# One attention and feed-forward block on one core: batch 1's projections behind the first scores, paired products in the spare bank, idle products, another order at the end

## What is computed

```python
x = x + xattn(layernorm(x), ctx)
x = x + ffn(layernorm(x))

def xattn(x, ctx):
    q, k, v, qc = x @ Wq + bq, x @ Wk + bk, x @ Wv + bv, x @ Wcq + bcq
    kc, vc = ctx @ Wck + bck, ctx @ Wcv + bcv
    y  = softmax(causal(q @ k.T * scale)) @ v        # per head
    y += softmax(qc @ kc.T * scale) @ vc
    return y @ Wp + bp

def ffn(x):
    w = top8(sigmoid(x @ Wr + br)), normalized       # [tokens, 32]
    shared = (silu(x @ Wg_s + bg_s) * (x @ Wu_s + bu_s)) @ Wd_s + bd_s
    routed = sum over e of w[:, e] * ((silu(x @ Wg[e] + bg[e]) * (x @ Wu[e] + bu[e])) @ Wd[e] + bd[e])
    return shared + routed
```

## Time and profile before

| | before |
|---|---|
| median of 3 runs | 218.98 us (217.91 to 220.17) |
| the profiled execution | 220.7 us |
| its span, first to last instruction | 218.4 us |
| its mean granted TensorE clock | 0.944 |
| busy: PE, DVE, ACT, POOL | 197.5, 165.4, 141.4, 94.2 us |
| share of the chain that ended last: PE, DVE, ACT, issue | 69%, 15%, 6%, 5% |

### The profile page before, as it was taken

One profiled execution on the slowest core, in us unless ns is written; L12 is line 12 of the kernel. 1 busy time (PEld: TensorE's weight loads), 2 busy tenths in 40 slices (PEclk: granted clock), 3 DMA queues, 4 the chain that ended last, 5 costly groups with the idle time before them and its releaser, 6 DMA issues.

```text
span 218.4 us, 3993 instructions
## 1 busy us (share of the span) xinstructions
PE 197.5 (90%) x1227; PEld 143.5 (66%) x1238; DVE 165.4 (76%) x378; ACT 141.4 (65%) x275; POOL 94.2 (43%) x148
## 2 busy tenths in 40 slices
PE   7884989898999999899898978679999999999983
PEld 2553776566776767676665646457888888887752
DVE  2988766367677898798765689796687887887982
ACT  3456465568689888898777693665567656555471
POOL 7799555024237365737646322524265233220000
PEclk9998555899999999999999999999999999999996
DMA  4264422102343324210211100000023000000003
GB/s 115 81 161 128 107 66 70 32 12 72 78 104 79 85 62 103 48 41 3 72 36 39 36 0 2 3 0 0 2 56 91 18 2 0 0 0 3 0 0 96
DMA packets 20433, 10.39 MB, mean 48 GB/s; under 512 B 11881, under 2 KB 18542, under 8 KB 20414
## 3 DMA queue, kind: packets, MB, share of 16 engines
q1 hardware_dynamic: 19290, 9.24, 16.8%
q0 software_dynamic: 672, 0.69, 1.3%
q10 hardware_dynamic: 452, 0.23, 0.5%
HBM read 4.51 MB, written 0.52 MB: 23 GB/s over the span
## 4 chain that ended last, share of the span: by engine, by line
PE 69%; DVE 15%; ACT 6%; issue 5%; POOL 2%; DMA 1%; DVEq 0%; POOLq 0%; ACTq 0%
PE psum L1268 12%; PE psum L1269 10%; PE psum L1270 10%; PE psum L1370 6%; PE psum L1439 3%; PE psum L1451 3%; PE psum L1416 3%; PE psum L1583 3%; PE psum L1421 3%; PE psum L1461 3%; PE psum L1369 3%; PE psum L1402 2%; POOL hid_lo L655 2%; PE psum L1390 2%; PE psum L1425 2%
## 5 line engine op out<-in xcount | busy, mean ns | idle before, releaser
L856 ACT ACTIVATE gate<-psum,bias_cols 128x512 f32<-128x512 f32 (+2 forms) x35 | 23.5, 674 | 30.3 <-PE psum L1270 30.3
L747 ACT ACTIVATE probs<-psum 128x512 f32<-128x512 f32 x64 | 36.8, 596 | 7.0 <-PE psum L1421 3.6
L1211 DVE SCALAR_TENSOR_TENSOR gated<-psum,bias_cols,gate 128x512 f32<-128x512 f32 x32 | 24.0, 749 | 10.5 <-ACT gate L856 10.4
L597 POOL TENSOR_TENSOR w_ffn_lo<-w_ffn,w_ffn_hi 128x384 fp32r<-128x384 f32 x17 | 20.7, 1218 | 25.8 <-ACT w_ffn_hi L761 25.8
L1268 PE MATMUL psum<-xT_hi,w_ffn_hi 128*128 128x512 f32 x66 | 26.9, 407 | 0.0
L1370 PE MATMUL psum<-key_blocks,query_rows 96*128 96x512 f32 x48 | 26.1, 586 | 0.2 <-ACT key_blocks L683 0.2
L1269 PE MATMUL psum<-xT_lo,w_ffn_hi 128*128 128x512 f32 x66 | 26.3, 398 | 0.0
L1270 PE MATMUL psum<-xT_hi,w_ffn_lo 128*128 128x512 f32 x66 | 25.9, 392 | 0.0
L621 POOL TENSOR_SCALAR_AFFINE_SELECT probs<-probs 128x512 f32<-128x512 f32 x16 | 10.2, 635 | 31.5 <-ACT probs L747 31.4
L1224 DVE TENSOR_TENSOR hid<-gated,psum 128x512 f32<-128x512 f32 x32 | 21.9, 683 | 1.2 <-POOL hid_lo L655 0.3
L863 ACT CAST hid_hi<-hid 128x512 fp32r<-128x512 f32 (+1 forms) x33 | 20.2, 612 | 1.8 <-DVE hid L1224 1.2
(11 more groups left out here) (179 smaller groups left out, 482.6 us busy)
## 6 DMA issues: line engine op xcount, KB each, us to landing
query_rows<-queries SPq DMA_DIRECT2D x46, 64.0 KB, 2.0
key_rows<-keys SPq DMA_DIRECT2D x39, 32.0 KB, 1.9
w_ffn<-in_L_ffn_Wg SPq DMA_DIRECT2D x16, 64.0 KB, 2.0
w_ffn<-in_L_ffn_Wu SPq DMA_DIRECT2D x16, 64.0 KB, 2.1
w_ffn<-in_L_ffn_Wd SPq DMA_DIRECT2D x16, 64.0 KB, 2.1
ckey_rows<-ckeys POOLq DMA_DIRECT2D x12, 32.0 KB, 2.0
key_rows<-keys POOLq DMA_DIRECT2D x9, 32.0 KB, 1.9
x_sb<-in_x SPq DMA_DIRECT2D x2, 128.0 KB, 2.7
```

Of the source, the lines that this page charges most:

```text
L597: ins = pool.tensor_tensor(w_ffn_lo[:, k, :, :], w_ffn[:, k, :, :], w_ffn_hi[:, k, :, :].bitcast(F32), ALU.subtract).then_inc(ffn_lo, 1)
L747: act.activation(probs[:, i % 2, c, :], bank(B_ST + c % 2), ACT.Exp, scale=SCALE).then_inc(exp_done, 1)
L856: act.activation(gate[rows_of(n), n % 3, part], psum[of, B_GATE + n % 2, part], ACT.Silu, bias=bias_cols[of, BIAS_GATE + u:BIAS_GATE + u + ...
L1211: dve.scalar_tensor_tensor(out=gated[:, n % 3, :], in0=bank(B_UP + n % 2), scalar=bias_cols[:, BIAS_UP + u:BIAS_UP + u + 1], in1=gate[:, n ...
```

## The change

1. **Opening.** `project(1)` moves from ahead of `natural(0)` to behind it, and makes the values first. On ACT, `expand(0)`, `expand_ctx(0)` and `expand(1)` move ahead of the three `round_qkc(1, n)`, and the four `norm` of batches 2 and 3 move from ahead of the loop to behind the first `exps`. On DVE `values(1)` moves between the maxima of step 0.
2. **Products in pairs.** The spare bank is used in halves: keys and queries of batches 2 and 3 are made together (`keys_queries`, steps 1 and 3), cross queries and values together (`cross_values`, steps 2 and 4), all ahead of `attend_context`. Nothing is made in `late_at` of steps 1 to 3 any more, and nothing in step 5. ACT waits for the second product of a pair before it reads the first.
3. **Idle products.** One more ahead of `turn_x(0)`, one more behind it, eight for five ahead of `natural(0)`, and two ahead of each of `turn_max(0)` to `turn_max(3)`, for which `take_misc` now stands ahead of the wait for the maxima.
4. **End.** The gate product of the last item (33) moves ahead of the down product of item 30, and `hid_lo` of item 31 goes from DVE to GpSimd.

```diff
-        tail_at = {0: [("x_pair", FIRST_BATCHES)], 1: [("qkc", 6)], 2: [("qkc", 8)],
-                   3: [("qkc", 9)], 4: [("qkc", 10)], 5: [("qkc", 11)]}
-        late_at = {1: [("qkc", 7)], 2: [("values", 2)], 3: [("values", 3)]}
+        tail_at = {0: [("x_pair", FIRST_BATCHES)]}
+        for b in range(FIRST_BATCHES, BATCH):
+            tail_at[2 * b - 3] = [("keys_queries", b)]
+            tail_at[2 * b - 2] = [("cross_values", b)]
+        late_at = {}
...
-        POOL_LO = [*range(8)]
+        POOL_LO = [*range(8), LAST_ITEM - 2]
...
-            return bank(B_QKC + n if b < FIRST_BATCHES else B_MISC, SEQ)
+            if b < FIRST_BATCHES:
+                return bank(B_QKC + n, SEQ)
+            half = n % 2
+            return psum[:, B_MISC, SEQ * half:SEQ * (half + 1)]
...
             def round_qkc(b, n):
                 bias = ORDER[n][1]
-                act.wait_ge(m_qkc, 3 * b + n + 1)
+                act.wait_ge(m_qkc, 3 * b + max(n, b >= FIRST_BATCHES) + 1)
...
-            run_idle(3, B_OUT)
+            run_idle(4, B_OUT)
             turn_x(0)
-            run_idle(1, B_OUT)
+            run_idle(2, B_OUT)
...
-            run_idle(5, B_CK)
-            project(1)
+            run_idle(8, B_CK)
...
             def turn_max(i):
 
+                if i == 0:
+                    pe.wait_ge(have_value, FIRST_BATCHES)
+                take_misc(shift_placed, i + 1)
+                if i < 4:
+                    run_idle(2, B_MISC)
                 pe.wait_ge(max_done, 3 * i + 3)
-                take_misc(shift_placed, i + 1)
...
             natural(0)
-            pe.wait_ge(have_value, FIRST_BATCHES)
+            project(1)
             turn_max(0)
             natural(1)
...
+                if n == LAST_ITEM - 1:
+                    project_gate(LAST_ITEM)
                 if n >= 2:
                     m = n - 2
```

More of the change, by code:

```diff
@@ L353, in product_bank, with value_bank @@
         def product_bank(b, n):
-            return bank(B_QKC + n if b < FIRST_BATCHES else B_MISC, SEQ)
+            if b < FIRST_BATCHES:
+                return bank(B_QKC + n, SEQ)
+            half = n % 2
+            return psum[:, B_MISC, SEQ * half:SEQ * (half + 1)]
+        def value_bank(b):
+            half = b >= FIRST_BATCHES
+            return psum[:, B_VALUE, SEQ * half:SEQ * (half + 1)]
         def lo_done(n):
@@ L656, in lower_half @@
                                    ALU.subtract).then_inc(pool_lo_done, 1)
-            for n in POOL_LO:
+            for n in POOL_LO[:-1]:
                 if ("project", BATCH - 1) in [beside.get((n, slot)) for slot in "ABC"]:
@@ L786, in norm @@
                                bias=neg_mean[:, t:t + 1]).then_inc(x_normed, 1)
-            expand(1)
             shift(0)
             expand_ctx(1)
-            act.wait_ge(have_neg_mean, 1)
-            for t in range(*NORM_GROUPS[2]):
-                norm(t)
             expand(2)
@@ L796, in _ @@
                 exps(i, (0,))
+                if i == 0:
+                    act.wait_ge(have_neg_mean, 1)
+                    for t in range(*NORM_GROUPS[2]):
+                        norm(t)
                 if i + 1 < STEPS:
@@ L1035, in maxima @@
                     tile_1()
+                    values(1)
                     dve.wait_ge(m_nat, 3)
@@ L1063, in tail @@
                     lo_half(xT_lo[:, CHUNK:TOKENS], bank(B_MISC), xT_hi[:, CHUNK:TOKENS], xT_split)
-                if name == "qkc":
-                    split_qkc(b // 3, b % 3)
+                if name == "keys_queries":
+                    split_qkc(b, 0)
+                    split_qkc(b, 1)
+                if name == "cross_values":
+                    split_qkc(b, 2)
+                    values(b)
                 if name == "y_turn":
@@ L1133, in _ @@
             expand_ctx(0)
-            values(1)
             maxima(0)
@@ L1162, in _ @@
                 for name, b in late_at.get(i, ()):
-                    if name == "values":
-                        values(b)
-                    if name == "qkc":
-                        tail(name, b)
+                    tail(name, b)
                 if i == 6:
@@ L1285, in project @@
                     pe.wait_ge(w_qkv_split, 1)
+                if b:
+                    pe.wait_ge(have_value, b)
+                    project_values(b)
                 for n in range(3):
@@ L1465, in tail @@
             def tail(name, b):
-                take_misc({"x_pair": xT_split, "qkc": qkc_split, "values": have_value, "y_turn": yT_split, "project": x1_ready,
-                           "x2_turn": x2T_split, "router": logits_ready,
-                           "route_turn": routeT_ready}[name], b + 1)
+                reader = {"x_pair": xT_split, "keys_queries": qkc_split, "cross_values": have_value, "y_turn": yT_split, "project": x1_ready,
+                          "x2_turn": x2T_split, "router": logits_ready,
+                          "route_turn": routeT_ready}[name]
+                take_misc(reader, 3 * b + 2 if name == "keys_queries" else b + 1)
                 if name == "x_pair":
@@ L1473, in tail @@
                     ins.then_inc(t_x, 1)
-                if name == "qkc":
+                if name == "keys_queries":
                     pe.wait_ge(xT_split, FIRST_BATCHES + 1)
-                    project_qkc(b // 3, b % 3)
-                if name == "values":
+                    project_qkc(b, 0)
+                    project_qkc(b, 1)
+                if name == "cross_values":
+                    project_qkc(b, 2)
                     project_values(b)
@@ L1553, in left_over, with project_gate @@
                     tail(name, b)
+            def project_gate(n):
+                u, c = WORK[n]
+                k = u % SLOTS
+                cols = slice(c * CHUNK, (c + 1) * CHUNK)
+                if u == 0:
+                    pe.wait_ge(x2T_split, 2 * c + 2)
+                pe.wait_ge(ffn_lo, u + 1)
+                if n >= 2:
+                    pe.wait_ge(gate_done, n - 1)
+                    if WORK[n - 2][0] == SHARED:
+                        pe.wait_ge(hid_done, n - 1)
+                product3(bank(B_GATE + n % 2), w_ffn_hi[:, k, 0, :], w_ffn_lo[:, k, 0, :], xT_hi[:, cols],
+                         xT_lo[:, cols]).then_inc(m_gate, 1)
             pe.wait_ge(b_down_split, 1)
@@ L1560, in _ @@
                     cols = slice(c * CHUNK, (c + 1) * CHUNK)
-                    if u == 0:
-                        pe.wait_ge(x2T_split, 2 * c + 2)
-                    pe.wait_ge(ffn_lo, u + 1)
-                    if n >= 2:
-                        pe.wait_ge(gate_done, n - 1)
-                        if WORK[n - 2][0] == SHARED:
-                            pe.wait_ge(hid_done, n - 1)
-                    product3(bank(B_GATE + n % 2), w_ffn_hi[:, k, 0, :], w_ffn_lo[:, k, 0, :], xT_hi[:, cols],
-                             xT_lo[:, cols]).then_inc(m_gate, 1)
+                    if n < LAST_ITEM:
+                        project_gate(n)
                     left_over(n, "A")
```

33 lines of the change are left out of this document (18 added, 15 removed).

## The result

| | before | after |
|---|---|---|
| median (range, runs) | 219.57 us (217.91 to 221.34, 4) | 212.95 us (212.52 to 213.56, 4) |
| ratio, 95% interval | | 0.9725 [0.9656, 0.9794] |
| the profiled execution | 220.7 us | 212.95 us |
| its span | 218.4 us | 211.1 us |
| its mean granted TensorE clock | 0.944 | 0.986 |

A forecast was written before the change was run, and what follows sets the result against it. TensorE's half clock in steps 0 and 1 was taken as the bound. Terms -0.5 - 1.15 - 2.1 - 3.4 - 0.6 - 0.7 = -8.45, off the median 218.98, gave 210.5 us; range 208.0 to 215.5.

The forecast's parts named there:

- What bounds the kernel: Opening: TensorE's clock at 1.2 GHz for 20.5 us, from 19.7 to 40.2, lies on the path in steps 0 and 1.
- The clock holds: Opening: the likeliest case, no fall to half clock, median 210.5 us as summed; chance 0.73.
- A: Opening up to natural(1): natural(0) starts 1.0 us earlier, natural(1) at 19.9; -0.5 us, bounds 0 and -1.0.
- B: natural(1): its seven matmuls run at full clock, 1.40 us for 2.55; -1.15 us, bounds 0 and -1.15.
- C: Step 0: 5.9 us at full clock for 7.97, idle pair 0.43 included; -2.1 us, bounds -1.2 and -3.1.
- D: Step 1: 6.8 us at full clock for 10.19; -3.4 us, bounds -2.8 and -4.7.
- E: Steps 2 to 5: two waits of 0.52 go (-1.04), idle products cost up to 0.43; net -0.6, bounds 0 and -1.0.
- F: End: item 32's down product loses its 1.02 us wait; -0.7 us, bounds 0 and -1.0.
- The signs: Right: natural(0) about 14.4, natural(1) 19.9, step 2 at 33 to 34; wrong: steps 0 and 1 over 7 us at full clock.
- All lower ends together: Whole kernel: every term's most favourable bound at once, put at 206.9 us.
- the clock falls as before: Opening rival: half clock from about 19.7 to 40, 218.7 us, no change; chance 0.09.
- The slower one: Opening rival: clock falls earlier, ahead of natural(0), before about 16; +2.4 us, 221.4; chance 0.05.

The follow-up runs named there:

- e3: The kernel before with five idle products ahead of turn_max(0) and five behind it, nothing moved: 214.89 us, ratio 0.9814.
- e6: e1 with GpSimd's context key blocks of step 3 (expand_ctx(3)) put ahead of its loop: 213.78 us, ratio 0.9861.
- e8: e6 with the four norm ahead of the loop again and five idle products ahead of the wait for x_norm: 214.37 us, ratio 0.9828.
- e1: The changed kernel without the two idle products ahead of each of the first four turned maxima: 212.26 us, ratio 0.969.
- e4: The changed kernel with the products of batches 2 and 3 made singly again, by the tables of before: 213.82 us, ratio 0.9765.
- e2: The kernel before with only the idle pairs ahead of the first four turned maxima, and take_misc ahead of the maxima wait: 215.86 us, ratio 0.9832.
- e5: The changed kernel with the end of before (gate product of item 33 and item 31's low half put back): 213.99 us, ratio 0.9894.
- e12: The kernel of e1 once more, on another chip with six executions: 212.78 us, ratio 0.9762.
- e14: e1 with five idle products between turn_max(0) and natural(1): 212.43 us, ratio 0.9729, one of five executions at 616.67.
- e11: The changed kernel with 13 idle products ahead of natural(0), five behind turn_max(0), pairs only for i < 2, e8's GpSimd and FFN edits: 213.03 us, ratio 0.975.
- e10: The changed kernel with the opening of before (values of batch 1 still first) and no added idle products: 216.80 us, ratio 0.9968.

## Why the prediction was right, and where it was off

- **What bounds the kernel: right.** The half clock in steps 0 and 1 was on the path. e3 takes it away with nothing moved and gains 5.85 at step 6. So the mechanism was right, not only the number.
- **The clock holds (0.73): right for the change, and less sure than the single trace made it look.** In none of the eight executions did it fall for long. But I read one execution of before as its constant behaviour; in a later job one of thirteen of it kept its clock, and two kernels with nearly the change's opening (e6, e8) lost part of it in five of eight. The case was a matter of odds within one kernel, which a chance for the whole kernel doesn't tell. The prediction also said that the trace shows no place between the opening's 3.15 us and waits of 0.5 to 0.7. It does: 1.39 us ahead of 138.87 and 1.25 us ahead of 146.36 (`route`), both at full clock.
- **A, 0.32 for 0.5.** `natural(0)` waited for DVE's blocks, as put, but until 14.69 and not 14.4: 0.7 earlier, of which the chain of maxima passed on the half.
- **B, 1.03 for 1.15. C, 2.36 for 2.1.** Right; the nearest full-clock rows carried over. The idle pair, charged with 0.43 in C, cost nothing: step 0 takes 5.61 with it and 5.62 without (e1), where the wait ahead of `natural(2)` is the longer for it. The `norm` were hidden, as e8 shows.
- **D, 3.02 for 3.4.** Step 1 took 7.17 for 6.8. What was late next is GpSimd: `ckey_blocks` for the context part of `natural(3)`, which at half clock had been in time. With them earlier it is 6.78 (e8). I had looked at DVE and ACT as next, not at GpSimd. The idle pair, which I charged with 0.43 here, hid in that wait.
- **E, 0.12 for 0.6.** The term that was mis-sized is the 1.04 for the two waits of 0.52, and with it "perhaps nothing to wait for". The idle products of step 2 cost 0.45, as charged, but the pairs brought only 0.2 in steps 2 to 5 (e4), because waits appeared ahead of the turned maxima of steps 3 to 5: 0.18 (42.42), 0.61 (48.83) and 0.18 (55.10) us, where before there was none. The rest is the order of the two waits in `turn_max`, 0.09 a step, which was in no term; e2 shows it for steps 3 to 6, and step 2 fits it (0.35 longer in e2 than before, where the pair costs 0.45). Over four steps that is 0.36, and 0.2 + 0.36 - 0.45 gives the 0.1.
- **F, 0.6 for 0.7.** The down product of item 31 does wait for GpSimd, 0.35 us, and the idle ahead of that of item 32 is gone.
- **What was not in the sum.** The dip at 133.7, which costs 0.5 in that execution; 0.4 at the last turning, which is the clock again; 0.2 in steps 6 to 14; and the time outside the span, shorter by 0.45. A to E came to 6.85 at step 6 for 7.75, 0.9 short, and partly by luck these make the whole difference 7.75 for 8.45.
- **The signs.** `natural(0)`, `natural(1)` and the down product of item 32 came as written. Step 2 started at 34.37, just outside 33 to 34, and step 1 took 7.17, which was written down as a sign of a bound by ACT or DVE; it was GpSimd's.
- **The arithmetic.** All lower ends together give 218.98 - 11.95 = 207.0, not 206.9. Nothing rests on it.
- **The base.** The terms explain 0.7 of the miss of 2.4. The rest, 1.7, is one step: I took the saving, worked out from a profiled execution 1.7 above the median, off the median. That execution was slow because its clock was at half for longer (0.944), and this is what the change removes; 220.7 - 8.45 = 212.25 would have been the consistent forecast. The two profiled executions differ by 7.75 us, the medians by 6.6.
- **Rivals.** That the clock falls as before happened in e6, not in the change. The slower one, a fall ahead of `turn_max(0)`, did occur in e5, e12 and e14, but for 3.4 us and at a cost of 0.5 to 1.0 us at step 6, not for the rest of the opening. I had priced a long fall, because the trace of before shows only that kind.

**Open.** What decides whether an execution falls, for 3.4, 17.1 or 20.5 us or not at all. Whether e6 and e8 fell more often than e1 because of GpSimd's edit or by chance: four executions each, on another chip, can't tell. Which part of the new opening holds the clock. Whether the idle pairs buy steadiness for their 0.45 (8 of 8 with them, 9 of 10 without, but e11 with two of them 4 of 6).

## What to carry to other kernels

Where a row of granted clock shows half speed on a path that TensorE sets, find the emptiest place just ahead of the fall and test it by filling it with products that nobody reads, before anything is moved; here that alone gave about five of the seven microseconds. Then give each execution's mean clock beside its time and take a saving off the time of the execution it was read from, since the median mixes executions that fell for long with ones that fell for less or not at all. And when a stretch gets faster, list every engine's due time in it, the idlest one's too: the next wait was GpSimd's.

## What the runs showed of the hardware that I had not expected

- The fall has several lengths: 20.5 us (before, e6, e10), 17.1 (e2) and 3.4 (the change at 133.7, e3 and e4 at 134.9 and 134.5; e5, e12 and e14 at 16.1 to 16.4), each read from windows of the granted clock, always between 2.4 and 1.2 GHz.
- The same program, with the same waits to 0.05 us up to the place, falls in one execution and not in another (e1 and e6, whose edit lies on GpSimd; e1 and e12, one kernel, whose profiled executions have no dip and one of 3.4 us; before, 214.74 us at 0.989 against 220.25 at 0.944).
- Products of zeros that nobody reads can keep the clock: ten in e3, in all four executions, at a cost of 0.09 us or less at `natural(1)`. It isn't sure: with both places filled, e11 still had two of six executions at 0.979 and 0.984.
